# Scores of three 16-wide attentions: from bf16 triples in 96 rows to rounded-f32 pairs in 48 rows, two heads in the two halves of TensorE's array

## The reference

```python
    q = (x @ wq).reshape(b, s, NH, HD)
    k = (x @ wk).reshape(b, s, NKV, HD)
    v = (x @ wv).reshape(b, s, NKV, HD)
    k = jnp.repeat(k, NREP, axis=2)
    v = jnp.repeat(v, NREP, axis=2)
    scores = jnp.einsum('bihd,bjhd->bhij', q, k) * SCALE
    ...
    scores = jnp.where(causal, scores, jnp.finfo(scores.dtype).min)
    attn = jax.nn.softmax(scores, axis=-1)
    out = jnp.einsum('bhij,bjhd->bihd', attn, v)
    out = out.reshape(b, s, NH * HD)
    return out @ wo
```

## Time and profile before

| | us |
|---|---|
| median of 3 runs | 2105.11 (2103.57 to 2106.55) |
| profiled execution | 2105.01 |
| its span | 2102.9 |
| TensorE busy | 1962.9 (93%) |
| VectorE busy | 1089.8 (52%) |
| ScalarE busy | 775.4 (37%) |
| GpSimd busy | 747.5 (36%) |

### The profile page before, as it was taken

How to read it: one execution, slowest core, us unless ns; L and a number is a source line. 1 busy time by engine, 2 the same in 40 slices (tenths; PEclk the granted TensorE clock), 3 DMA queues, 4 the chain that set the end, 5 groups by cost and what they waited for, 6 DMA issues and landing times.

```text
span 2102.9 us, 28210 instructions
## 1 busy us (share of the span) xinstructions
PE 1962.9 (93%) x10552; PEld 1245.9 (59%) x10552; DVE 1089.8 (52%) x1971; ACT 775.4 (37%) x1647; POOL 747.5 (36%) x1203
## 2 busy tenths in 40 slices
PE   5899967999999999999999899979999997999897
PEld 3454435777777777777776687844444454544443
DVE  4666466555555555555555324135556354566345
ACT  1565523333333333333333233322455402565411
POOL 1455315434343434343432344322344312343300
PEclk9899979999999999999999899999999998999998
DMA  7223000101010101010100234115333006111101
GB/s 196 39 40 104 2 20 1 51 1 51 1 51 1 51 1 51 1 50 1 51 1 30 76 106 170 46 29 64 47 62 102 31 1 77 32 33 46 52 0 40
DMA packets 46200, 95.01 MB, mean 45 GB/s; under 512 B 7689, under 2 KB 35721, under 8 KB 43017
## 3 DMA queue, kind: packets, MB, share of 16 engines
q1 hardware_dynamic: 43474, 90.86, 16.9%
q10 hardware_dynamic: 2592, 2.36, 0.7%
HBM read 62.20 MB, written 2.10 MB: 31 GB/s over the span
## 4 chain that ended last, share of the span: by engine, by line
PE 83%; DVE 7%; ACT 2%; DMA 2%; issue 2%; POOL 1%; ACTq 1%; POOLq 0%; SPq 0%; DVEq 0%
PE PS L1365 11%; PE PS L1434 9%; PE PS L1417 7%; PE PS L1390 7%; PE PS L444 5%; PE PS L547 5%; PE PS L1776 5%; PE PS L525 5%; PE PS L491 5%; PE PS L572 3%; PE PS L1402 3%; PE PS L1376 3%; PE PS L1789 3%; PE PS L1747 2%; PE PS L459 2%
## 5 line engine op out<-in xcount | busy, mean ns | idle before, releaser
L965 ACT ACTIVATE PB<-PS 128x512 f32<-128x512 f32 x480 | 281.5, 600 | 240.6 <-PE PS L525 237.7
L741 DVE TENSOR_REDUCE NM<-PS 128x2 f32<-128x1024 f32 x192 | 209.2, 1091 | 185.7 <-PE PS L493 184.6
L870 POOL TENSOR_SCALAR_AFFINE_SELECT PB<-PB 128x256 f32<-128x256 f32 (+1 forms) x480 | 174.2, 367 | 322.9 <-ACT PB L965 316.9
L1564 ACT COPY PRT<-PS 128x512 f32<-128x512 f32 (+3 forms) x256 | 108.9, 426 | 415.6 <-PE PS L1402 409.8
L491 PE MATMUL PS<-KQ 96*128 96x512 bf16 (+3 forms) x768 | 189.1, 311 | 46.4 <-DMA KQ<-LOW 31.6
L1524 DVE TENSOR_REDUCE NX<-PS 128x1 f32<-128x512 f32 (+3 forms) x256 | 124.3, 490 | 171.2 <-PE PS L1391 169.2
L1677 POOL TENSOR_SCALAR PR<-PR,RCP 128x512 f32<-128x512 f32 (+3 forms) x256 | 135.7, 535 | 201.4 <-DVE RCP L1512 194.8
L525 PE MATMUL PS<-KQ 99*128 99x512 bf16 (+3 forms) x768 | 183.8, 305 | 5.6 <-DMA KQ<-NMT 2.5
L1390 PE MATMUL PS<-kT,qT 128*128 128x512 f32 (+3 forms) x512 | 184.0, 441 | 4.3 <-ACT PR L1622 4.1
L444 PE MATMUL PS<-XTT,WA 128*128 128x512 f32 x288 | 146.8, 617 | 13.5 <-DVE ident_masks_b L2314 12.0
L1622 ACT ACTIVATE PR<-PS,NX 128x512 f32<-128x512 f32 (+3 forms) x256 | 136.5, 533 | 46.9 <-DVE NX L1524 45.7
(11 more groups left out here) (285 smaller groups left out, 3965.7 us busy)
## 6 DMA issues: line engine op xcount, KB each, us to landing
KQ<-HI SPq DMA_DIRECT2D x90, 128.0 KB, 4.0
KQ<-MID SPq DMA_DIRECT2D x72, 128.0 KB, 4.7
WB<-f_w SPq DMA_DIRECT2D x12, 768.0 KB, 4.4
WB<-w1o SPq DMA_DIRECT2D x8, 1024.0 KB, 7.9
WC<-f_w SPq DMA_DIRECT2D x10, 768.0 KB, 4.4
WB<-w1a SPq DMA_DIRECT2D x8, 768.0 KB, 4.4
WB<-w1b SPq DMA_DIRECT2D x8, 768.0 KB, 5.9
WA<-w SPq DMA_DIRECT2D x6, 1024.0 KB, 6.4
```

The source lines that it names most:

```text
L741: x = dve.tensor_reduce(nm[:, h:h + 2, i], PS[:, b:b + 2, 0:(i + 1) * P], AX.X, ALU.max, negate=True)
L870: pool.affine_select(blocks, blocks, [[0, count], [1, P]], ALU.is_ge, 0.0, base=0, channel_multiplier=-1).then_inc(s16["probs_ready"].sem, 1)
L965: act.activation(PB[:, n % PBS, :], PS[:, 4 + n % 2, :], ACT.Exp, scale=self.scale)\
```

## The change

**Numbers and layout.** A chunk is split in two parts in TensorE's rounded f32 form (F32R), HI by ScalarE and LOW by VectorE (the old REST); MID and GpSimd's LOW go. Three products of parts stay, in 48 rows. `KQ` is f32 with half as many heads per 512 columns: even heads of a group in rows 0 to 47, odd heads in rows 64 to 111. `row` issues two transfers for each row block, one per half; where keys are shared (L0, L3) the whole key chunk goes to both halves. The maxima are split in two, f32, in rows 48 and 49 of each half.

**TensorE.** Each score matmul names its half (`tile_position=(64 * par, 0)`). In the loop, each `scoresT` block of one half is followed by the `scores` block of the same width in the other. A mask, which needs 128 rows, is made of two matmuls over 64 rows in each half. Units are five per group instead of six. PV stands in one piece in slot 3, behind `max_T` (now in bank 6, with the projections), `back` in slot 7, and other work in blocks in slots 5 and 7 (some in 8).

**Others.** VectorE does `turn`, `take` and the tails' `mean` at the start of a step (`ahead`). HI buffers move. The ones come from a tile that a memset fills, so the first transfer waits for it.

```diff
-SR = 6 * HD
-MR = 3
+SR = 3 * HD
+MR = 2
...
-PASS1 = ((3, 0, 2), (0, 0, 4), (3, 2, 4), (2, 0, 2), (2, 2, 4), (1, 0, 4))
+UNITS = (((3, 0, 0),), ((3, 1, 0),), ((2, 0, 0), (0, 0, 384)), ((2, 1, 0), (0, 1, 384)), ((1, 0, 0), (1, 1, 256)))
...
-                    pe.matmul(ps, KQ[0:SR, self.query(G, h), i * P:(i + 1) * P],
-                              KQ[0:SR, self.key(G, h), 0:n], start=True, stop=False)
-                    x = pe.matmul(ps[:, n - P:n], identb[:, :], mask_qk[:, :], start=False, stop=True)
-                x.then_inc(s16["scores_ready"].sem, 1)
+                i, j, at = UNITS[a][x]
+                n, rows = (i + 1) * P, slice(64 * par, 64 * par + SR)
+                pe.matmul(PS[:, 2 * (u % 2) + par, at:at + n], KQ[rows, self.query(G, j), i * P:(i + 1) * P],
+                          KQ[rows, self.key(G, j), 0:n], start=(x == 0), stop=False, tile_position=(64 * par, 0))
+
+            def masks(self, pe, G, a):
+
+                u = NUNIT * G + a
+                for x, (i, j, at) in enumerate(UNITS[a]):
+                    for half in range(2):
+                        for par in (1, 0):
+                            rows, far = slice(64 * par, 64 * par + 64), 2 * (half != par)
+                            to = slice(at + i * P + 64 * half, at + (i + 1) * P)
+                            ins = pe.matmul(PS[:, 2 * (u % 2) + par, to], ident_masks_b[rows, far, :],
+                                            ident_masks_b[rows, far + 1, 64 * half:P], start=False,
+                                            stop=(half == 1 and x == len(UNITS[a]) - 1), tile_position=(64 * par, 0))
+                ins.then_inc(s16["scores_ready"].sem, 1)
...
                 on = self.on
                 pe.wait_ge(on["max_parts"].sem, on["max_parts"].at(G + 1))
-                pe.transpose(PS[0:MR * 16, 3, 0:P // 2].bitcast(BF16), NM3[:, G % 2, :], identb[:, :])\
+                pe.wait_ge(*self.aux)
+                pe.transpose(PS[0:MR * 16, AUX, 0:P], NM2[:, G % 2, :].bitcast(F32), ident[:, :])\
                   .then_inc(s16["maxT_psum"].sem, 1)
...
+                if s in self.late and k in (5, 7):
+                    for c in range(2):
+                        self.project(pe, self.late[s], c + k - 5)
...
                     for k in range(10):
-                        self.scoresT(pe, s, k)
-                        self.aside(pe, s, k)
-                        if more and k in (0, 1, 2, 5, 6, 7):
-                            self.scores(pe, s + 2, (0, 1, 2, 5, 6, 7).index(k))
+                        for x in range(len(self.blocks(k))):
+                            self.scoresT(pe, s, k, x)
+                            if more:
+                                self.scores(pe, s + 2, k // 2, 1 - k % 2, x)
+                        if more and k % 2:
+                            self.masks(pe, s + 2, k // 2)
                         if k == 1 and s >= 3 and s % 2:
                             self.ctx_T(pe, (s - 3) // 2, 7)
-                        if k == 3 and s + 1 < last:
-                            self.max_T(pe, s + 1)
-                        if 3 <= k <= 5 and s:
-                            self.pv(pe, s - 1, k - 3)
-                        if k == 8 and s:
+                        if k == 3:
+                            if s + 1 < last:
+                                self.max_T(pe, s + 1)
+                            if s:
+                                for part in range(3):
+                                    self.pv(pe, s - 1, part)
+                        if k == 7 and s:
                             self.back(pe, s - 1)
+                        self.aside(pe, s, k)
...
+            def ahead(self, dve, st, s):
+
+
+                t = s - self.out_step
+                if s - 1 in self.late:
+                    self.turn(dve, self.late[s - 1]) if self.rope else self.take(dve, self.late[s - 1])
...
+                if 0 <= t - 1 < NT:
+                    self.tails[0].mean(dve, st, t - 1, PS[:, AUX, :])
...
-            def middle(self, act, m):
-
-                on = self.on
-                act.wait_ge(on["rest_ready"].sem, on["rest_ready"].at(m + 1))
-                act.copy(MID[:, m % 3, :], REST[:, m % 2, :]).then_inc(s16["mid_ready"].sem, 1)
...
+            def row(self, eng, m, r, part):
+
+                b, kind, i = self.chunks[m]
+                a, n = (self.query(2 * NC * b + 2 * i, 0), 4) if kind == "q" else \
+                    (self.key(2 * NC * b + 2 * i, 0), 4 if self.wide else 8)
+                for par in range(2):
+                    to = slice(64 * par + r * HD, 64 * par + (r + 1) * HD)
+                    eng.dma_start(KQ[to, a:a + n, :].bitcast(F32), (part[par::2, :] if n == 4 else part).bitcast(F32))\
+                       .then_inc(s16["rows%d_loaded" % (m % 3)].sem, 16)
...
+            sp.wait_ge(start.sem, 1)
             sp.dma_start(XTT[:, 0], d["xT"][0]).then_inc(S_xT[0].sem, 16)
```

## The result

The changed kernel takes **2164.6 us** (median of four runs, 2162.5 to 2164.9) against 2105.1 for the kernel before: a ratio of **1.028, interval 1.026 to 1.030**. The forecast was 2063. The profiled execution spans 2162.8 us against 2102.9, so 59.9 us have to be found.

A forecast was written before the change was run, and what follows sets the result against it. The prediction took TensorE to set the pace in the loops, ScalarE and VectorE coming next. From 2105 us it took 40 for the loops and 2 ahead of them: 2063 us, own range 2045 to 2075, chance 0.38.

The forecast's parts named there:

- Overlap of the halves: Score pairs and masks on TensorE: matmuls in two row halves run side by side, 2.1 us less TensorE work per step.
- rival E: Every score pair and mask: halves don't overlap, +1.3 us in 31 steps, +0.6 in 15, 10 ahead; 2165 us, chance 0.12.
- A pair's price: Score pairs on TensorE: 0.23, 0.175, 0.12 and 0.107 us by width; with masks 3.23 us per step against 5.37.
- What the step gives back: Loop steps: ScalarE runs dry in blocks, 1.4 of 2.1 us return as waits; projection steps 11.7 us, others 9.2.
- The -30 for projection steps: Loop steps with a projection: -1.3 us in each of 23 (7 in L3, 5 in L0, 11 in L2).
- The -1.1 in each of the first steps: Three first steps, counted among those without a projection: -1.1 us by the same sum, part of -6.
- L0's rotation steps: L0's steps 5, 7, 9: VectorE gets the subtraction beside its rotation, 9.6 us, no gain; same in steps 2 and 3.
- the output steps: Output steps of each stage: mean ahead of the maxima, their transpose waits for the same bank; -0.3, -0.9, -0.9, -6 in all.
- Last two steps: Last two steps of a stage: nothing to pair across and 8 more switches, +2 us in all.
- Ahead of the loops: Before the three loops: row transfers +4, first two groups' savings, memset wait +0.3; -2 us (-15 to +16).
- Rival F: TensorE's clock falls with more waits: +2.1 us in every step gives 2160, in a third of them 2095; chance 0.08.
- rival C: Loop blocks starve ScalarE less (-28) and transfers ahead are packet-bound (-8): 2030 us, chance 0.12.

The follow-up runs named there:

- Experiment 10: Changed kernel with each slot's plain scores in the same array half as its transposed ones: 2216.7 us, one run.
- e10_half_blocks: Changed kernel with transfers of ones behind the first four chunks' rows, plus L2's steps 0 to 2 projecting in halves after slots 5, 6, 8, 9: 2141.9 us.
- Experiment 6: Changed kernel with ones behind the rows, leaving out the half multiplications with the sine for five chunks rotated in L0's loop (computation incomplete): 2131.8 us.
- experiment 3: Changed kernel with ones behind the rows, plus L0's and L3's first key chunk sent even heads first, odd heads behind the first queries: 2136.6 us.
- experiment 5: Unread matmuls keep TensorE busy: ahead of the rows on the changed kernel, 2167.0 us; through both first groups too, on experiments 1, 3 and 4, 2125.2 us.
- e2_keep_busy: Changed kernel with 80 matmuls of 512 columns that nobody reads ahead of the wait for the first key and query rows: 2167.0 us.
- experiments 1, 3 and 4: Changed kernel with ones behind the rows, even key heads first, and chunk 4's projection piece by piece behind units 0 to 3: 2135.7 us.
- e13_busy_ahead: On experiments 1, 3 and 4: unread matmuls ahead of L0's and L3's first rows, after first two groups' units and before first transposed scores: 2125.2 us.
- e3_same_half: Changed kernel with plain scores taking the same array half as the slot's transposed ones: 2216.7 us, one run.

## Why the prediction was wrong, step by step

**Overlap of the halves.** Right. The measured 2164.6 is by chance the number of rival E (2165), whose mechanism did not happen: partners start together. A time that fits a rival proves nothing without its row.

**A pair's price.** Mis-sized. I took the stream's 0.23, 0.175, 0.12 and 0.107 us; by starts a pair of 512 columns takes 0.34 behind a wait or a change of shape. Read over the step at 1924.08, pairs and masks come to about 4 us against 3.23. The Trainium skill (TensorE: Matmul & The Clock Gate, Part 3) has loads run beside matmuls in flight only where the row group differs. The trace agrees for partners, whose loads start 3 or 4 ns apart as a rule, but it shows more: the loads of the second pair start at 1925.66, while the first pair, in the same two row groups, is in flight since 1925.55. None of this helps the first pair of a slot, where nothing is in flight.

**What the step gives back.** The mechanism (waits for exponents) was right, its size nearly: forecast 11.7 and 9.2 us for steps with and without a projection, measured 12.2 and 9.3. The -30 for projection steps should have been -18 on undisturbed steps. Experiment 10 says how little of TensorE's scores still set the pace: 0.2 to 0.5 us more per step at the full clock for four pairs taken apart. The -1.1 in each of the first steps did not come: L2's steps 0 to 2 alone cost 7.3 us more, a loss that no experiment but e10_half_blocks touched.

**L0's rotation steps.** "9.6, no gain" was 10.5 with the full clock and 12.1 to 13.1 without. VectorE's sum there is 9.0 us in the row; what I missed is that TensorE waits at the transpose of the maxima, which now shares its bank with the projection, until the rotation has read it: 5.2 us in five steps, and the clock falls with it. Experiment 6 prices all of it at 6 us by the medians and 10.7 in the profiled loop. The same bank undid the output steps: for them I had -6 in all, and they took 0.6 us more.

**Last two steps.** "+2 in all" was +3.7 per stage, 11 in all. I counted switches and forgot the exposed load.

**Ahead of the loops.** The step that failed most: -2 became +39. I weighed bytes, packets and queues of the rows, and put the transfers of ones at nothing; all that the sum has of them is the memset that initial loads wait for (+0.3). Their shape was in the diff: two partitions, 512-byte runs, first in the queue. They cost 27 us, more than any other term. The Trainium skill (DMA: Bandwidth & Descriptors, "Why a DMA increments its semaphore by 16 and not by 1") says that a transfer runs on as many engines, up to 16, as divide the slowest dimension of its patterns, on this path the lowest-numbered ones. For a leading dimension of 2 that gives two engines, and two parts of each transfer were late. By the same rule the kernel before used three engines for its ones, with 16 KB on each; now each of two gets 64 KB in L0 and L3, as much as four key transfers of 256 KB give it. An estimate from that: at the 136 GB/s of the earlier trace rows, shared by 16 engines, 64 KB take 7.7 us of the 10. So the bytes per engine may be most of it, and how much the short runs add no run here shows. Of the rest, bytes alone are not the cause: experiment 3 brought the first scores back to the old time, but then the first two groups take 24 us to the first exponent instead of 17 to 19. The clock takes part in the first steps (experiment 5).

**The clock.** Rival F had 0.08 and was in the right direction: half-clock time rose from 143 to 238 us. That total is no price, since TensorE stands idle in the part of it that falls into the waits for rows (e2_keep_busy took it to 200 without a gain). Keeping TensorE busy ahead of and in the first groups, on top of experiments 1, 3 and 4, brings it from 204 to 149 and the time from 2136 to 2125. I had seen the old first steps at 0.83 and 0.81 and written that more waits would make this worse, and still gave it no place in the sum.

**A slip in rival C.** Its two terms, -28 and -8, make 2027, not 2030; neither is near the measured time.

**What stays open.** In e13_busy_ahead, with about as much half-clock time as the kernel before, 20 us remain. In its profiled execution, 18.6 us longer than the kernel before, they are 11.9 in L2's loop (7.3 of them in its steps 0 to 2), 3.3 in L0's, 10.1 in the later loop starts of L0 and L3, less 2.5 in L3's loop and 4.2 between the loops of L0 and L2. The last two steps of the three stages are 11 of the loops' share. Why the first groups still need 23 to 24 us to the first exponent, with the rows there and the clock mostly full, was not settled; candidates are the second lot of rows and the maxima's transfer behind it, and neither was tried alone.

## What to carry to other kernels

Look at the shape of every transfer that a change adds, above all the small ones at the head of a queue: one that reaches two partitions can hold back what stands behind it for as long as these two take, while a count of all bytes calls it free. Count the bytes per partition. When work is taken off the bounding engine, ask what it does in the freed time: waits next to the clock's half level turn saved microseconds into lost ones. And price a packed matmul by the distance between starts behind a wait, with its weight load, not by its stream.

## What the runs showed of the hardware that was not expected

- Two transfers of 64 KB (2 partitions, runs of 512 bytes) put two of the 16 parts of each of the transfers behind them up to 10 us late in L0 and L3; two of 48 KB in L2 up to 5. One of the two in front gave 10.6 of 26.8 us of wait. The issue of the transfers behind them took up to 2.9 us each on ScalarE's queue, against at most 1.2 without them.
- Row halves of TensorE (48 or 50 rows each) start their matmuls and their loads 3 or 4 ns apart in most pairs; where the two come from different slots (e3_same_half, step 4 of L3), 8 to 22 ns.
- The same step of the same code took 12.94 us at the full clock and 14.52 at a mean of 0.88. Which steps were hit changed from kernel to kernel; that some were did not.
- Matmuls ahead of a wait did not keep the clock up behind it: with 80 of them ahead of L0's first scores, the clock was full until 53.0 us and from 59.8 to 66.6, and the 23.9 us over the first steps were at half again.
